# A Mamba block with a gated network on one core: norms by ScalarE, two additions by GpSimd, a second accumulator in the last stage, and seven scan units of sixteen driven by TensorE

## The reference, cut to what matters

```
mod = (silu(c) @ wmod).reshape(16, 6, 1, -1)      # sa, ca, ga, sb, cb, gb per sequence
h  = layernorm(x) * (1 + ca) + sa
xn = layernorm(h, ln1)
x1 = mamba(xn, m1);  x2 = flip(mamba(flip(xn), m2))
x  = x + ga * (layernorm(x1 + x2, ln2) + xn)
h  = layernorm(x) * (1 + cb) + sb
x  = x + gb * ffn(h)

mamba: xz = x @ W_in.T; xc = silu(conv4(xp) + b); dt = softplus(..); A = -exp(A_log)
       h_t = exp(dt_t * A) * h_(t-1) + (dt_t * xc_t) * B_t      # 512 channels x 64 states
       y_t = sum over states of h_t * C_t;   (y + xc * D) * silu(z) @ W_out.T
ffn:   h = silu(x @ w1) * (x @ w2);  h = gelu(h @ h1);  h = gelu(h @ h2);  h @ w3
```

## Time and profile before

| what | value |
|---|---|
| median of 3 runs | 13444.66 us (13441.17 to 13444.91) |
| the profiled execution | 13442.57 us |
| its span, first to last instruction | 13440.8 us |
| busy share of the span | VectorE 93%, GpSimd 85%, ScalarE 80%, TensorE 76% |
| granted TensorE clock, mean | 0.877 |
| first and last unit scanned | from 167.7 us to 13147.0 us |

### The profile page before, as it was taken

The page is one execution under the profiler, slowest core; times in us unless marked ns, Lnnn a source line. Parts: engine busy times, 40 slices in busy tenths (PEclk is TensorE's granted clock), DMA queues, the critical chain, the costliest instruction groups (busy, mean ns, idle before and its releaser), DMA issues.

```text
span 13440.8 us, 178922 instructions
## 1 busy us (share of the span) xinstructions
PE 10269.7 (76%) x51228; PEld 5835.9 (43%) x51228; DVE 12440.7 (93%) x7383; ACT 10728.5 (80%) x23196; POOL 11452.0 (85%) x5812
## 2 busy tenths in 40 slices
PE   5567877778787787877878777787877878778776
PEld 2234444444344444434444444443444444344445
DVE  5999999999999999999999999999999999999991
ACT  5788878888887887878888788888878878788882
POOL 4898888888888888888988888888888888889892
PEclk7778988889898898988989888898988989889898
DMA  2223333333333333333333333333333333333332
GB/s 84 79 88 106 107 106 118 116 102 117 98 121 106 110 118 103 119 103 114 118 106 107 106 118 116 104 118 96 122 106 112 116 102 119 103 114 120 102 108 87
DMA packets 605372, 1450.00 MB, mean 108 GB/s; under 512 B 68400, under 2 KB 109504, under 8 KB 599792
## 3 DMA queue, kind: packets, MB, share of 16 engines
q1 hardware_dynamic: 604272, 1437.26, 32.8%
HBM read 1346.70 MB, written 90.31 MB: 107 GB/s over the span
## 4 chain that ended last, share of the span: by engine, by line
PE 26%; ACT 25%; issue 21%; DVE 17%; POOL 11%; DMA 0%; DVEq 0%; POOLq 0%; ACTq 0%; SPq 0%
DVE state L1227 9%; ACT v_sb L1047 8%; ACT state L1034 8%; PE driven L857 8%; POOL state L1257 8%; PE y_ps L871 5%; PE q_ps L812 5%; DVE driven L1216 3%; PE q_ps L799 2%; PE p_ps L720 2%; PE b_ps L847 1%; ACT L1034 1%; POOL v_sb L1320 1%; PE p_ps L728 1%; ACT hid L1017 1%
## 5 line engine op out<-in xcount | busy, mean ns | idle before, releaser
L1257 POOL TENSOR_TENSOR state<-state,c_rep 128x1024 f32<-128x1024 f32 x4096 | 9661.5, 2382 | 1544.2 <-DVE state L1227 1543.4
L1227 DVE TENSOR_TENSOR_SCAN state<-state,driven 128x1024 f32<-128x1024 f32 x4096 | 9105.9, 2270 | 462.7 <-PE driven L857 245.8
L1047 ACT ACTIVATE v_sb<-u_t,b_t 128x128 f32<-128x128 f32 x12288 | 3978.2, 505 | 1764.3 <-PE driven L857 1759.3
L1034 ACT ACTIVATE state<-ud_rep,cols_sb 128x512 f32<-128x512 f32 x8192 | 5175.6, 709 | 3.0 <-DMA ud_rep<-ud_rows 0.8
L857 PE MATMUL driven<-consts_sb,v_sb 128*128 128x128 f32 x16384 | 2700.5, 319 | 2119.8 <-DVE state L1227 2089.2
L857 PEld LDWEIGHTS driven<-consts_sb,v_sb 128*128 128x128 f32 x16384 | 2184.9, 164 | 3778.6 <-DVE state L1227 2605.4
L871 PE MATMUL y_ps<-state,consts_sb 128*32 128x512 f32 x16384 | 2523.6, 693 | 372.1 <-POOL state L1257 369.4
L1216 DVE TENSOR_TENSOR driven<-ud_rep,b_ps 128x1024 f32<-128x1024 f32 x2048 | 2390.0, 1212 | 17.0 <-DMA ud_rep<-ud_rows 17.0
L812 PE MATMUL q_ps<-hid,wq_sb 128*128 128x256 f32 x8192 | 2132.6, 406 | 241.1 <-ACT hid L1012 152.2
L812 PEld LDWEIGHTS q_ps<-hid,wq_sb 128*128 128x128 f32 x8192 | 1534.3, 197 | 982.8 <-issue 750.2
L1320 POOL TENSOR_TENSOR v_sb<-u_t,b_t 128x512 f32<-128x512 f32 x1024 | 1181.7, 1154 | 11.4 <-ACT u_t L963 11.4
(11 more groups left out here) (121 smaller groups left out, 5616.7 us busy)
## 6 DMA issues: line engine op xcount, KB each, us to landing
c_rep<-bc_rows SPq DMA_DIRECT2D x2048, 256.0 KB, 3.0
ud_rep<-ud_rows SPq DMA_DIRECT2D x512, 512.0 KB, 4.1
wq_sb<-in_h SPq DMA_DIRECT2D x512, 512.0 KB, 3.8
wq_sb<-in_f SPq DMA_DIRECT2D x128, 512.0 KB, 4.0
wp_sb<-in_win SPq DMA_DIRECT2D x64, 512.0 KB, 4.8
dt_sb<-conv_taps SPq DMA_DIRECT2D x32, 1024.0 KB, 5.6
ud_rows<-u_pad SPq DMA_DIRECT2D x128, 256.0 KB, 3.5
ud_rows<-dt_sb SPq DMA_DIRECT2D x128, 256.0 KB, 3.4
```

The costliest lines, as they stand in the source:

```text
L1034: ins = act.activation(state[:, unit % STATE_RING, j, :], ud_rep[:, nth % 2, j, 1, :], ACT.Exp, scale=a_neg[:, d, c, j, g:g + 1])
L1047: ins = act.activation(v_sb[:, unit // 2 % V_RING, tt, :, :, n].rearrange("p j e -> p (j e)"), u_t[:, nth % 2, tt, :], ACT.Identity, scale ...
L1227: dve.tensor_tensor_scan(flat, flat, driven[:, q % DRIVE_RING].rearrange("p j t -> p (j t)"), 0.0, ALU.mult, ALU.add).then_inc(scanned, 1)
L1257: pool.tensor_tensor(part, part, c_rep[:, unit % ROW_RING, :].unsqueeze(1).to_broadcast([P, 2, T]), ALU.mult).then_inc(was_read, 1)
```

## The change

Five things change.

1. The `_norm` step goes from VectorE to ScalarE: x * rstd + (-mean * rstd), with scale and bias per partition. GpSimd computes -mean * rstd in two more small instructions. `x_scale` and `mix` on VectorE, the transposes after a norm on TensorE and the store of `xa` on SyncE wait for ScalarE now.
2. `mix1` and the additions at `W0` and `W1` go from VectorE to GpSimd, as `mixed`, `add0` and `add1`. What follows waits for GpSimd there.
3. Of sixteen units TensorE now drives seven, numbers 1, 3, 6, 8, 10, 13 and 15, and VectorE nine. So units 4 and 5, and 11 and 12, are two in a row by VectorE, as are none before.
4. ScalarE writes the three pieces of `v_sb` for unit U in iterations U-4, U-3 and U-2, one in each, between the two halves of the decays of another unit.
5. In `tail`, the steps of the network alternate between `q_ps` and `p_ps`, and `bank_free` looks two steps back.

```diff
-DRIVE_RING, STATE_RING, ROW_RING, V_RING, V_AHEAD, POOL_AHEAD = 2, 4, 2, 2, 5, 3
-PE_UNITS = tuple(range(1, UNITS, 2))
-DVE_UNITS = tuple(range(0, UNITS, 2))
+DRIVE_RING, STATE_RING, ROW_RING, V_RING, V_AHEAD, POOL_AHEAD = 2, 4, 2, 2, 4, 3
+CYCLE, PE_OF_CYCLE = 16, (1, 3, 6, 8, 10, 13, 15)
...
-    dve = [(s, part, name + "_stats", TT), (s + 1, part, name + "_aggr", TT), (s + 3, part, name + "_norm", TT)]
+    dve = [(s, part, name + "_stats", TT), (s + 1, part, name + "_aggr", TT)]
...
-    return [(s + 2, part, name + "_rstd", 7)], dve
+    return [(s + 2, part, name + "_rstd", 9)], [(s + 3, part, name + "_norm", TT)], dve
...
-    dve += [(MIX_AT + i, "early", f"mix{i}", 1) for i in range(2)]
+    dve.append((MIX_AT, "early", "mix", 1))
+    pool.append((MIX_AT + 1, "early", "mixed", 1))
...
-        dve.append((w_at + 4, part, f"W{i}", 2))
+        dve.append((w_at + 4, part, f"W{i}", 1))
+        pool.append((w_at + 4, part, f"add{i}", 1))
...
+def by_pe(unit):
+    return unit % CYCLE in PE_OF_CYCLE
...
+        def q_bank(at, part, name):
+
+            if at.kind != "tail":
+                return q_ps
+            return (q_ps, p_ps)[[s[1:3] for s in PE_Q if at.has(s[1]) and s[3]].index((part, name)) % 2]
...
-                if j:
-                    p, n = steps[j - 1][1:3]
+                back = 2 if at.kind == "tail" else 1
+                if j >= back:
+                    p, n = steps[j - back][1:3]
...
# TensorE, iteration `unit`
-                    to_drive, ends_pass = scans and unit + 1 in PE_UNITS, unit % NG == 0
+                    to_drive, ends_pass = scans and unit + 1 < UNITS and by_pe(unit + 1), unit % NG == 0
...
-                        if unit + 2 < UNITS:
-                            spread(at, unit + 2)
-                        elif at.has("next"):
-                            spread(at, unit + 2)
+                    if not by_pe(unit + 2) and (scans if unit + 2 < UNITS else scans and at.has("next")):
+                        spread(at, unit + 2)
...
# ScalarE
+                if name.endswith("norm"):
+                    i = 0 if part == "next" else 1
+                    src, dst = {"o": (o_sb, o_sb), "n": (x_q, o_sb), "x": (xa, xa), "h": (xa, xa)}[name[0]]
+                    act.wait_ge(pool_side.sem, pool_side.done(at, part, name[0] + "_rstd"))
+                    for tt in range(TT):
+                        act.activation(dst[:, tt, :], src[:, tt, :], ACT.Identity, scale=rstd[:, i, tt:tt + 1],
+                                       bias=less_mean[:, i, tt:tt + 1]).then_inc(done, 1)
...
-                    if unit % 2 == 0:
-                        if in_scan(at, unit + 2):
-                            decays(at, unit + 2, 0)
-                            decays(at, unit + 2, 1)
-                        if in_scan(at, unit + V_AHEAD):
-                            make_v(at, unit + V_AHEAD, 0)
-                    else:
-                        if in_scan(at, unit + V_AHEAD - 1):
-                            make_v(at, unit + V_AHEAD - 1, 1)
-                        if in_scan(at, unit + 2):
-                            decays(at, unit + 2, 0)
-                            decays(at, unit + 2, 1)
+                    if in_scan(at, unit + 2):
+                        decays(at, unit + 2, 0)
+                    for tt in (2, 1, 0):
+                        ahead = unit + V_AHEAD - tt
+                        if by_pe(ahead) and in_scan(at, ahead):
+                            make_v(at, ahead, tt)
+                    if in_scan(at, unit + 2):
+                        decays(at, unit + 2, 1)
                     side(at, unit)
...
# VectorE
-                    elif name[2:] == "norm":
-                        dve.wait_ge(pool_side.sem, pool_side.done(at, part, kind + "_rstd"))
-                        for tt in range(TT):
-                            emit(dve.tensor_scalar(dst[:, tt, :], src[:, tt, :], mv[:, i, tt, 0:1],
-                                                   rstd[:, i, tt:tt + 1], ALU.subtract, ALU.mult), tt == TT - 1)
...
-                elif name == "mix1":
-                    dve.wait_ge(pool_side.sem, pool_side.done(at, "early", "pre2"))
-                    emit(dve.tensor_tensor(x_q[:], x_q[:], o_sb[:], ALU.add), True)
...
-                    emit(dve.tensor_tensor(dst, dst, tmp, ALU.add))
...
# GpSimd
+                    emit(pool.tensor_tensor(nb, mean, r, ALU.mult))
+                    emit(pool.tensor_tensor(nb, zero.to_broadcast([P, TT]), nb, ALU.subtract))
...
+                    pool.wait_ge(dve_side.sem, dve_side.done(at, part, f"W{i}"))
+                    dst = x_q[:, 2 * i:2 * i + 2, :]
+                    pool.tensor_tensor(dst, dst, hid2[:, 0:2, :], ALU.add).then_inc(done, 1)
...
+                    pool.wait_ge(dve_side.sem, dve_side.done(at, part, "mix"))
+                    pool.tensor_tensor(x_q[:], x_q[:], o_sb[:], ALU.add).then_inc(done, 1)
```

More of the change, by code:

```diff
@@ L170, with pe_units, dve_units @@
 CHUNKS = chunks()
+def by_pe(unit):
+    return unit % CYCLE in PE_OF_CYCLE
+def pe_units(unit):
+    return unit // CYCLE * len(PE_OF_CYCLE) + sum(k < unit % CYCLE for k in PE_OF_CYCLE)
+def dve_units(unit):
+    return unit - pe_units(unit)
 class At:
@@ L583, in store_xn @@
             def store_xn(at):
[L584 removed]
+                wait(act_side.sem, act_side.done(at, "next", "h_norm"))
                 sp.dma_start(rows_of(xn_dram, at.b + 1), xa[:]).then_inc(xn_out.sem, 16)
@@ L599, in store_out @@
             def store_out(at):
-                wait(dve_side.sem, dve_side.done(at, "late", "W1"))
+                wait(pool_side.sem, pool_side.done(at, "late", "add1"))
                 sp.dma_start(rows_of(out, at.b - 1), x_q[:]).then_inc(out_stored.sem, 16)
@@ L1000, in step @@
                     m = int(name[2])
+                    if m == 0 and (name[1] == "1" or at.kind != "first"):
+                        act.wait_ge(pool_side.sem, pool_side.done(at, "early", "add0") if name[1] == "1"
+                                    else pool_side.before(at))
                     for which, hid in enumerate((hid1, hid2)):
-                        act.activation(hid[:, m, :], q_ps[:, which * TH:(which + 1) * TH], ACT.Identity,
+                        act.activation(hid[:, m, :], q_bank(at, part, name)[:, which * TH:(which + 1) * TH], ACT.Identity,
                                        scale=scales[:, which, m:m + 1]).then_inc(done, 1)
@@ L1221, in scan @@
                 dve.wait_ge(decayed, of_body(at, HALVES, q + 1))
-                if unit in DVE_UNITS:
+                if not by_pe(unit):
                     dve.wait_ge(dve_driven, dve_drives(at, unit, h))
@@ L1238, in body @@
                         scan(at, 2 * unit + 1)
-                        if unit + 1 < UNITS and unit + 1 in DVE_UNITS or unit + 1 == UNITS and at.has("next"):
+                        if not by_pe(unit + 1) and (unit + 1 < UNITS or at.has("next")):
                             drive(at, unit + 1, 0)
@@ L1330, in body @@
                     ahead = unit + POOL_AHEAD
-                    if unit % 2 == 0 and (at.kind in SCAN_PARTS if ahead < UNITS else at.has("next")):
+                    if by_pe(ahead) and (at.kind in SCAN_PARTS if ahead < UNITS else at.has("next")):
                         make_v(at, ahead)
```

106 lines of the change are left out of this document (58 added, 48 removed).

## The result

The changed kernel takes 13135.74 us, median of 4 runs (13133.56 to 13139.53), against 13443.57 us of the kernel before on the same chip (4 runs, 13441.17 to 13444.91): a ratio of 0.9772, 95% interval 0.9755 to 0.9788. The forecast was 13215. The profiled execution has a span of 13134.3 us, 306.5 less than before. By stages: a body of the loop takes 795.3 us instead of 815.7, the body `first` 799.1 instead of 791.8, and the tail after the last scan 259.7 instead of 293.8. The first scan starts at 168.6 us instead of 167.7.

A forecast was written before the change was run, and what follows sets the result against it. The prediction took VectorE to bound the kernel, busy 778.5 of 815.8 us a body. Its terms, -105 - 33 - 110 + 50 - 34 + 2 = -230 us, gave 13213 us (13215 for the median), range 13100 to 13420.

The forecast's parts named there:

- Work that leaves VectorE: Norms and three additions leave VectorE, their time blocked on ports going with them: -415 us.
- the port time stays: Rival: GpSimd's port hold moves to VectorE's remaining instructions, only unblocked price saved: +57 us, 13502 us; chance 0.03.
- Work that comes: VectorE drives nine units of sixteen instead of eight, 256 more instructions at 1.212 us: +310 us.
- Waits for the norms: VectorE's waits for GpSimd's `_rstd` nearly vanish as norms go to ScalarE: -33 us, between -35 and 0.
- Waits for the decays: Most of VectorE's 160.8 us of waits for ScalarE's decays go: -110 us, between -161 and +50.
- Waits for the transposes: VectorE's waits for TensorE's transposes: fewer units and unit 13 save, low clock costs; net +50 us, between -60 and +306.
- Tail: After the last scan, two accumulators shorten network steps to 3.5 and 1.8 us: net -34 us, between -20 and -42.
- First body of projections: The first body of projections, counted apart from the loop, gets slower: +2 us.
- A body: One loop body takes about 803 us, VectorE busy 772, waiting near 3 for decays and near 17 for transposes.
- The clock decides: Rival: TensorE falls to 1.2 GHz wherever VectorE has two units in a row: +136 us, 13579 us; chance 0.15.
- The wait only moves: Rival: late last `v_sb` piece turns all decay waits into transpose waits: -120 us, 13325 us; chance 0.14.

The follow-up runs named there:

- norms_only: The kernel before with only the norms moved to ScalarE: 13131.3 us, ratio 0.9773.
- adds_only: The kernel before with only `mix1` and the additions of `W0` and `W1` moved to GpSimd: 13296.7 us, ratio 0.9895.
- sum_last_12: Changed kernel, TensorE driving every odd unit, `v_sb` pieces one iteration sooner, decays before the piece; in iteration 12 the sum behind both halves of transposes: 12907.6 us.
- pieces_sooner: The changed kernel with each piece of `v_sb` written one iteration sooner (U-5 to U-3), still seven units by TensorE: 13047.7 us, ratio 0.9709.
- the old shares: The changed kernel with TensorE's units and ScalarE's order of before; norms, additions and accumulators stay changed: 12993.2 us, ratio 0.9669.
- one_bank: The changed kernel with one accumulator in the tail instead of two: 13179.6 us, ratio 0.9804.
- sum_last_all: As sum_last_12, but with the sum behind both halves of transposes in every iteration where TensorE drives a unit, except pass ends: 12933.3 us.

## Why the prediction came out right

The time was in the range, 36 us above its lower end, and the sign and the main cause were right. That the sum fits to 79 us is in part luck: the waits for transposes came 71 us dearer than forecast, and all the rest some 150 us cheaper in sum. By its steps:

- *Work that leaves VectorE*, -415: right. norms_only shows it for the norms (334 us of busy time for 312), adds_only for the additions. The change in blocking of instructions that stay gave another 48 us in the kernel after. The rival *the port time stays* is refuted.
- *Work that comes*, +310: 299 measured. The forecast took the mean of 1.212 us for each; in pairs, as they stand, two take 2.33 us.
- *Waits for the norms*, -33: 44.2 - 11.3 = 33. ScalarE's norm instruction takes 589 ns, where 474 were priced, 29 us in all on an engine that is 79% busy.
- *Waits for the decays*, -110: -154. The term was too small.
- *Waits for the transposes*, +50: +121, the step that failed. It was -31 for one unit in eight less, -21 for unit 13 and +100 for the low clock behind two VectorE units in a row.
  - Unit 13 went from 21.5 to 38.6 us, +17 instead of -21. I took it that the wait would go with the norm's gap on VectorE. What came in its place is GpSimd's backlog: in norms_only the wait there is 3.62 us against 1.40, because TensorE's sum waits for GpSimd with the transposes behind it, and in sum_last_12 it is gone once the sum stands behind them. What makes GpSimd late, the pause of VectorE that is gone or the two more small instructions, was not run apart.
  - The clock behind such pairs is a small part. Second halves at units 6 and 13 of a cycle wait 103 us in all, 39 of them at unit 13, and they wait in 89 of 256 places. With the pieces sooner the same pairs stand in the kernel, and all waits for transposes are 226 us, fewer than the 307 of the old shares.
  - The last piece of `v_sb` at U-2, which I named as a risk inside the decays' term, has 140 us of these waits and 88 us of time to itself (pieces_sooner).
- *Tail*, -34: 293.8 to 259.7, and 44 us by one_bank; periods 3.53 and 1.73 where 3.5 and 1.8 were said.
- *First body of projections*, +2: the first scan starts 0.9 us later.
- *A body*: 795.3 us with VectorE busy 765, where 803 and 772 were said; at unit 13 the wait is above the 1.4 us that I gave as its end. The waits for the decays are 0 where 3 were said, those for the transposes 22 where 17 were.

Put together by groups, the forecast had parts 1, 2 and 5 at -415 - 33 - 21 - 34 + 2 = -501 us and parts 3 and 4 at +310 - 110 - 31 + 100 = +269. Measured are 12993.2 - 13440.9 = -448 and +143. The first is too hopeful by the transposes, whose waits rose from 246 to 307 us where -21 was said. The second is too dark: VectorE's busy time rose by 243 us instead of 310 (12004.4 to 12247.5), and the decays gave 149 back. There the transposes' +59 is near the -31 + 100 forecast by luck, since the late piece stood in for the clock.

VectorE's own account over the span closes the sum. Its busy time fell by 193 us: -423 of norms and additions, +299 of drives, -48 of other instructions that stayed, +6 of scans, and -27 of overlap (neighbouring instructions overlap a little; the rows added up exceed the busy time by 195 us before and by 222 after). Its idle time fell by 113 us: -33 for the norms, -154 for the decays, +121 for the transposes, -31 for the network in the tail, -16 for all else. No term of the forecast had the -48, the -27 and the -16.

*The clock decides* didn't come true. It had TensorE at 1.2 GHz in all 256 places; for the transposes of the second halves there it was so in 55 (a mean granted clock under 0.75). A low clock is seen at most waits, but was so before: ahead of 207 of the 247 us that VectorE waits at second halves the granted clock was under 0.7 over 1.5 us, and ahead of 146 of 182 us in the kernel before. *The wait only moves* was true in part: wholly at unit 29, while over the span 154 us left the decays and 121 came to the transposes. In pieces_sooner, without the late piece, nothing of the 121 is left (226 us against 246 before).

## What to carry to other kernels

- Price an instruction that leaves the busiest engine at its duration in the trace, waiting for ports included: that is what goes. Its neighbours on the same ports may shift by tens of us either way.
- Where two engines are near each other's pace (VectorE 93% busy, GpSimd 86 to 90%, each with work for the other), a wait can be backlog, and then it reappears behind the next thing in order, as in sum_last_12 and sum_last_all. Before an in-order stream is reordered, look at what the late instruction itself waits for.
- Where a producer runs ahead into a ring, try its lead by itself: one iteration was worth 88 to 157 us here, and it is one constant.

## What was not expected of the hardware

- Of VectorE's instructions with two SBUF inputs, the same one takes 3395 or 4428 ns on the mean, or 2982, by the kernel around it; nothing of it was changed.
- Nine small norm instructions on GpSimd take 3.3 us from the first to the end of the last, one of them, a power on 128x4 elements, 1.01 us by itself. Four multiplications in a row later GpSimd is still behind.
- ScalarE's activation on 128x256 with scale and bias per partition takes 583 to 601 ns with SBUF on both sides, against 467 ns on the mean from PSUM into SBUF in the first layer's steps.
- What stays open: seven of sixteen costs 66 us or 135, as the pieces are late or early. The traces say in which terms, but no run says why. Nor did any kernel here keep TensorE's clock up without giving it work in its order.
